# Sparse attention, select stage: key transposes of the next gathered batch behind the scores, second query pair behind them, division by the sums one batch later

## What is computed

```python
I = jnp.einsum('bth,bhts->bts', iw, logits)      # index scores of every token pair
I = jnp.where(causal, I, NEG)
vals, idx = jax.lax.top_k(I, TOPK)               # 32 keys per token
valid = vals > NEG / 2
q = (x @ wq).reshape(B, S, H, hd)                # 16 heads of 128
k = x @ wk                                       # one key and one value per token
v = x @ wv
k_sel, v_sel = gather(k, idx), gather(v, idx)
scores = jnp.einsum('bthd,btkd->bhtk', q, k_sel) * hd ** (-0.5)
scores = jnp.where(valid[:, None], scores, NEG)
p = jax.nn.softmax(scores, axis=-1)
o = jnp.einsum('bhtk,btkd->bthd', p, v_sel)
return o.reshape(B, S, H * hd) @ wo
```

## Time and profile before

| | |
|---|---|
| three runs | 3225.93, 3227.54, 3230.31 us; median 3227.54 |
| the profiled execution's own time | 3237.2 us |
| its span, first to last instruction | 3235.4 us |
| TensorE busy over the span | 2675.0 us (83%) |
| VectorE, ScalarE, GpSimd busy | 1769.7 (55%), 1487.8 (46%), 1052.4 us (33%) |
| mean granted TensorE clock | 0.911 |
| the loop of the select stage | about 2320 to 3058 us |

### The profile page before, as it was taken

One profiled execution on the slowest core, in us unless ns is written; L12 is line 12 of the kernel. 1 busy time (PEld: TensorE's weight loads), 2 busy tenths in 40 slices (PEclk: granted clock), 3 DMA queues, 4 the chain that ended last, 5 costly groups with the idle time before them and its releaser, 6 DMA issues. The chain is left out here.

```text
span 3235.4 us, 41872 instructions
## 1 busy us (share of the span) xinstructions
PE 2675.0 (83%) x14686; PEld 2043.5 (63%) x14686; DVE 1769.7 (55%) x3107; ACT 1487.8 (46%) x2915; POOL 1052.4 (33%) x943
## 2 busy tenths in 40 slices
PE   4967899899899895867989898888587877887788
PEld 4755455555555554756867676777576766766577
DVE  6456755656646736455357989898222233333443
ACT  2435457456456452333249868687333333233232
POOL 2542212102103101542314424242344445555222
PEclk9988999999999995988989999999788888899799
DMA  4241000000000003240010000000222222222100
GB/s 136 77 132 40 7 14 21 10 27 8 15 21 13 4 1 106 73 129 19 0 40 1 1 7 1 7 1 8 100 64 66 63 69 79 70 75 81 63 1 26
DMA packets 68367, 135.42 MB, mean 42 GB/s; under 512 B 16720, under 2 KB 38056, under 8 KB 66896
## 3 DMA queue, kind: packets, MB, share of 16 engines
q0 software_dynamic: 26048, 70.91, 7.4%
q1 hardware_dynamic: 42128, 61.96, 5.8%
HBM read 113.73 MB, written 18.71 MB: 41 GB/s over the span
## 5 line engine op out<-in xcount | busy, mean ns | idle before, releaser
L2138 POOL DMA_INDIRECT KV<-kv_scratch,sidx x384 | 368.3, 959 | 384.8 <-PE ps L2011 198.3
L1347 ACT ACTIVATE PT<-ps 128x512 f32<-128x512 f32 (+3 forms) x640 | 313.2, 534 | 321.3 <-PE ps L1098 178.9
L1213 DVE TENSOR_REDUCE xn<-ps 128x1 f32<-128x1024 f32 (+7 forms) x384 | 332.5, 907 | 112.6 <-PE ps L1074 85.9
L35 PE MATMUL ps<-KIh,qih 128*128 128x512 f32 (+2 forms) x640 | 252.6, 395 | 64.2 <-DVE Isc L1766 37.3
L36 PE MATMUL ps<-KIl,qih 128*128 128x512 f32 (+2 forms) x640 | 243.9, 381 | 0.0
L37 PE MATMUL ps<-KIh,qil 128*128 128x512 f32 (+2 forms) x640 | 243.4, 380 | 0.0
L1766 DVE SCALAR_TENSOR_TENSOR Isc<-ps,iw,Isc 128x1024 f32<-128x1024 f32 (+7 forms) x216 | 208.7, 966 | 56.5 <-ACT ps L1679 50.8
L1095 PE MATMUL ps<-qB,KB 128*128 128x512 f32 (+2 forms) x640 | 237.8, 372 | 0.0
L1679 ACT ACTIVATE ps<-ps,iwa 128x1024 f32<-128x1024 f32 (+7 forms) x240 | 198.0, 858 | 65.2 <-PE ps L37 64.5
L2114 DVE TENSOR_REDUCE smx<-ps 128x4 f32<-128x512 f32 (+3 forms) x92 | 61.0, 663 | 259.8 <-PE ps L1990 134.7
L2065 ACT ACTIVATE sP<-ps,snm 128x128 f32<-128x128 f32 (+2 forms) x256 | 101.2, 405 | 218.0 <-DVE snm L2117 170.0
(11 more groups left out here) (349 smaller groups left out, 7170.4 us busy)
## 6 DMA issues: line engine op xcount, KB each, us to landing
cs<-in_rope SPq DMA_DIRECT2D x20, 512.0 KB, 4.3
w1raw<-in_w SPq DMA_DIRECT2D x16, 512.0 KB, 4.1
ycomb<-y_rows SPq DMA_DIRECT2D x16, 512.0 KB, 4.9
KV<-kv_scratch,sidx POOLq DMA_INDIRECT x384
w2raw<-in_w SPq DMA_DIRECT2D x16, 256.0 KB, 5.2
xn_rows<-xnr SPq DMA_DIRECT2D x8, 512.0 KB, 4.1
whr<-in_whead SPq DMA_DIRECT2D x16, 256.0 KB, 3.0
wir<-in_wi SPq DMA_DIRECT2D x1, 2176.0 KB, 8.2
```

Of the source, the lines that this page charges most:

```text
L35: pe.matmul(out, lhs[0], rhs[0], start=start, stop=False)
L1213: v.tensor_reduce(mp[:, CT * h + r, k:k + 1], o[:, 0:end], AX_X, ALU.max).then_inc(a_free, 1)
L1347: s.activation(PT[:, rnd % 2, hh, lo:CH], ps[:, ST_BANKS[e % 3], lo:CH], ACT.Exp, scale=SCALE).then_inc(a_exp, 1)
L2138: g.indirect_dma_start(KV[:, BG * (k % RB) + m, :], None, a["kv_scratch"], bass.IndirectOffsetOnAxis(sidx[:, t % 2, at:at + 1], 0)).then_i ...
```

## The change

Three edits, in the loops of three engines.

- The key transposes become a function `turn_keys(batch)`. The first gathered batch's are made ahead of the loop; those of every other one are made in the iteration before its own (`after(n_)` gives the next batch if it is gathered), behind the scores and ahead of the output and of the product with the values. On ScalarE the two copies into `KT` (`turned_keys`) move in the same way, behind the exponentials of the iteration before and ahead of the copy into `oT`.
- Where a batch has two query pairs, the second is computed behind the scores and behind the key transposes, and on ScalarE copied behind the exponentials.
- On VectorE the reciprocal and the multiplications of batch `n_ - 1` stand in iteration `n_`, behind the copy into `sPT` and ahead of the maximum of batch `n_`.

```diff
--- before.py
+++ after.py
@@ -1914,6 +1914,9 @@
         def landed(batch):
             return 1 + 2 * GNUM[batch]
 
+        def after(n_):
+            return BATCHES[n_ + 1] if n_ + 1 < NBAT and BATCHES[n_ + 1][0] == "G" else None
+
         def w_piece(m):
             return slice(NHQ // 2 * m, NHQ // 2 * (m + 1))
 
@@ -1956,17 +1959,19 @@
                 queries(PAIRS[k], 6 + k % 2)
             pe.wait_ge(s_w[0], 32)
             pe.wait_ge(s_qe, FIRST_PAIRS)
+            def turn_keys(batch):
+                g = GNUM[batch]
+                pe.wait_ge(s_g[g % RB], 16 * BG * (g // RB + 1))
+                pe.wait_ge(s_kte, landed(batch))
+                for k in range(BG):
+                    i = pe.transpose(ps[:, k // 4, (k % 4) * P:(k % 4 + 1) * P], KV[:, BG * (g % RB) + k, 0:P], ident[:])
+                    if k % 4 == 3:
+                        i.then_inc(s_kt, 1)
+
+            turn_keys(BATCHES[0])
             for n_ in range(NBAT + LAG + 1):
                 batch = BATCHES[n_] if n_ < NBAT else None
                 old = n_ - LAG
-                if batch and batch[0] == "G":
-                    g = GNUM[batch]
-                    pe.wait_ge(s_g[g % RB], 16 * BG * (g // RB + 1))
-                    pe.wait_ge(s_kte, landed(batch))
-                    for k in range(BG):
-                        i = pe.transpose(ps[:, k // 4, (k % 4) * P:(k % 4 + 1) * P], KV[:, BG * (g % RB) + k, 0:P], ident[:])
-                        if k % 4 == 3:
-                            i.then_inc(s_kt, 1)
                 if 0 <= old < NBAT:
                     count, wide = groups(BATCHES[old])
                     pe.wait_ge(s_p, old + 1)
@@ -1974,7 +1979,7 @@
                     for j in range(count * wide // P):
                         i = pe.transpose(ps[:, 4, j * P:(j + 1) * P], sP[:, old % (LAG + 1), j, :], ident[:])
                     i.then_inc(s_pt, 1)
-                for pair in PAIRS_AT.get(n_, []):
+                for pair in PAIRS_AT.get(n_, [])[0:1]:
                     pe.wait_ge(s_qe, PAIR_NO[pair])
                     queries(pair, 6)
                 if batch:
@@ -2000,6 +2005,11 @@
                             pe.matmul(o, qD[:, h0 + h, P * (t % 2):P * (t % 2 + 1)], dK[:, 0:wide], start=h == 0, stop=False)
                             i = pe.matmul(o, far[:], dmb[:, 0:wide], start=False, stop=h == count - 1)
                         i.then_inc(s_s, 1)
+                if after(n_):
+                    turn_keys(after(n_))
+                for pair in PAIRS_AT.get(n_, [])[1:]:
+                    pe.wait_ge(s_qe, PAIR_NO[pair])
+                    queries(pair, 6)
                 for t in OUT_AT.get(n_, []):
                     output(t)
                 if 0 <= old < NBAT:
@@ -2044,16 +2054,18 @@
 
             for k in range(FIRST_PAIRS):
                 queries(PAIRS[k], 6 + k % 2)
+            def turned_keys(batch):
+                for k in range(2):
+                    s.wait_ge(s_kt, landed(batch) + k + 1)
+                    if GNUM[batch] >= 1:
+                        s.wait_ge(s_s, NUMBER[GATHERED[GNUM[batch] - 1]] + 1)
+                    s.copy(KT[:, 4 * k:4 * k + 4, :], ps[:, k, :]).then_inc(s_kte, 1)
+
+            turned_keys(BATCHES[0])
             for n_ in range(NBAT + LAG):
                 batch = BATCHES[n_] if n_ < NBAT else None
                 old = n_ - LAG
-                if batch and batch[0] == "G":
-                    for k in range(2):
-                        s.wait_ge(s_kt, landed(batch) + k + 1)
-                        if GNUM[batch] >= 1:
-                            s.wait_ge(s_s, NUMBER[GATHERED[GNUM[batch] - 1]] + 1)
-                        s.copy(KT[:, 4 * k:4 * k + 4, :], ps[:, k, :]).then_inc(s_kte, 1)
-                for pair in PAIRS_AT.get(n_, []):
+                for pair in PAIRS_AT.get(n_, [])[0:1]:
                     queries(pair, 6)
                 if batch:
                     count, wide = groups(batch)
@@ -2065,6 +2077,10 @@
                         i = s.activation(flat[:, wide * m:wide * (m + 1)], ps[:, 2 + n_ % 2, wide * m:wide * (m + 1)], ACT.Exp,
                                          bias=snm[:, at, m:m + 1], scale=SSC, accum_out=ssum[:, at, m:m + 1])
                     i.then_inc(s_ex, 1)
+                if after(n_):
+                    turned_keys(after(n_))
+                for pair in PAIRS_AT.get(n_, [])[1:]:
+                    queries(pair, 6)
                 if 0 <= old < NBAT:
                     last = BATCHES[old]
                     t = last[1]
@@ -2106,21 +2122,24 @@
                     v.wait_ge(s_pt, old + 1)
                     v.wait_ge(s_o, old)
                     v.tensor_copy(sPT[:, 0:count * wide // P, :].rearrange("p m k -> p (m k)"), ps[:, 4, 0:count * wide]).then_inc(s_pte, 1)
+                if 1 <= n_ < NBAT + 1:
+                    count, wide = groups(BATCHES[n_ - 1])
+                    at = (n_ - 1) % (LAG + 1)
+                    flat = sP[:, at].rearrange("p m k -> p (m k)")
+                    v.wait_ge(s_ex, n_)
+                    v.reciprocal(srs[:, at, 0:count], ssum[:, at, 0:count]).then_inc(s_rs, 1)
+                    v.wait_ge(s_rs, n_)
+                    for m in range(count):
+                        i = v.tensor_scalar(flat[:, wide * m:wide * (m + 1)], flat[:, wide * m:wide * (m + 1)], srs[:, at, m:m + 1], None, ALU.mult)
+                    i.then_inc(s_p, 1)
                 if batch:
                     count, wide = groups(batch)
                     at = n_ % (LAG + 1)
-                    flat = sP[:, at].rearrange("p m k -> p (m k)")
                     v.wait_ge(s_s, n_ + 1)
                     v.tensor_reduce(smx[:, at, 0:count], ps[:, 2 + n_ % 2, 0:count * wide].rearrange("p (m k) -> p m k", k=wide), AX_X,
                                     ALU.max).then_inc(s_nm, 1)
                     v.wait_ge(s_nm, 2 * n_ + 1)
                     v.tensor_scalar(snm[:, at, 0:count], smx[:, at, 0:count], -SSC, None, ALU.mult).then_inc(s_nm, 1)
-                    v.wait_ge(s_ex, n_ + 1)
-                    v.reciprocal(srs[:, at, 0:count], ssum[:, at, 0:count]).then_inc(s_rs, 1)
-                    v.wait_ge(s_rs, n_ + 1)
-                    for m in range(count):
-                        i = v.tensor_scalar(flat[:, wide * m:wide * (m + 1)], flat[:, wide * m:wide * (m + 1)], srs[:, at, m:m + 1], None, ALU.mult)
-                    i.then_inc(s_p, 1)
                 for t in OUT_AT.get(n_, []):
                     v.wait_ge(s_y, OUT_NO[t] + 1)
                     v.tensor_tensor(X[:, t, :], ps[:, 7, 0:D], X[:, t, :], ALU.add).then_inc(s_x, 1)
```

## The result

Four runs of each: 3207.5 us (3201.4 to 3210.7) against 3228.9 (3225.9 to 3233.7); ratio 0.9942, interval 0.9914 to 0.9971. The change is faster by 18.7 us, between 9 and 28, where 64 were forecast. The time lies in the range, near rival (a); three tenths of the forecast gain came.

The account below looks back on a forecast made before the run. TensorE was taken as nearest to the bound in the select loop, leaking through idle time, low clock and stalls. From 3237.2 us, -43 -10 -8 +12 -15 = -64 gave 3173.2, or 3163.5 against the runs' median; range 3110 to 3215.

Parts of the forecast that it names:

- rival (a): Select loop: TensorE's wait moves to the gather, at +47 and no clock gain; 3213 us, chance 15%.
- part 4: Key transposes want gathered rows earlier; perhaps eight more batches late by 1.5 us each: +12 us, bounds 0 and +47.
- three signs of being wrong: Over 60 us of DMA waits, clearly more "remote" waits, or over 30 us new before gathered scores for the KT copy.
- part 1: Dense product's wait for VectorE's copy shrinks; -43 us after 8 off for the last eight gathered batches, bounds -53 and -20.
- part 2: Second query pair behind the scores finds ScalarE's copy done: eight times 1.2 us, -10 us, bounds -27.3 and 0.
- part 3: TensorE's smaller waits, for the mask and before output products, shrink: -8 us, bounds -21 and 0.
- part 5: TensorE's clock spends less time at the lower level as idle time falls: -15 us, bounds -40 and 0.
- Rival (b): Slower: late key transposes hold up an output and a product needing no gathered row; 3269.5 us, chance 7%.
- Rival (c): Nothing: time saved between two stalls is given back in the next; within 6.5 us of 3227.5, chance 6%.
- Rival (d): The clock comes back as well, at -40, with larger savings on TensorE's waits: -113 us, 3114.5 us, chance 17%.

Follow-up runs that it names:

- e9: The whole change, but with key transposes behind the output product instead of ahead of it: 3215.1 us against 3225.3 for the kernel before, ratio 0.9967.
- e16: The kernel before with only the division moved one batch later: 3208.0 us against 3226.7, ratio 0.9938.
- e6: The whole change, unchanged, run where the kernel before takes 3068.4 us: 3107.1 us, ratio 1.0121.
- e10 to e12: Whole change, transposes behind output, last query pair behind value product; then also old division, or earlier first four gathers: 3226.2, 3228.8, 3229.7 us against 3225.3.
- e5: The kernel before, unchanged, profiled again where it takes 3068.4 us: 3070.3 us, ratio 1.0004.
- e15: The kernel before with each indirect gather exchanged for a plain DMA of 128 rows (output differs): 3051.9 us against 3226.7, ratio 0.9468.

## Why the prediction was wrong

The step that failed is part 4, the gather: +12 forecast, +53 measured. Two of the prediction's three signs of being wrong appeared, over 60 us of DMA waits (61.1) and clearly more "remote" waits (83 to 130 us); the third, a new wait before the gathered scores, stayed at 14.3 us. TensorE's idle time by line gives the terms as they came, in the first pair of traces (dense product, L35, outputs and mask, key transposes, gathered scores):

| term | forecast | measured |
|---|---|---|
| part 1, copy ahead of division | -43 | 61.1 to 8.2: -53 |
| part 2, second pair | -10 | 27.3 to 10.9: -16 |
| part 3, small waits | -8 | 14.3 to 5.7 and 8.2 to 5.8: -11 |
| part 4, gather | +12 | 7.7 to 61.1: +53 |
| part 5, clock | -15 | 0.87 to 0.87: 0 |
| not foreseen, gathered scores | 0 | 10.4 to 14.3: +4 |
| sum | -64 | -23 (stage -28, runs -19) |

**Parts 1 to 3 were right as waits**, in mechanism and nearly in size; part 1 came out at its far bound of -53. What I deducted from it for the last eight batches was not lost there. As time they did not come: the division alone is worth 19 us under A and 5 under B, and only with half the gather does the whole change give 36.

**Part 4 is the step that failed.** It was outside even its bound of +47, and it failed in three places. First, the slack was read from one pair: 5.4 us between landing and use, in a pair that a stall had stretched. Under B, where nothing is stalled, before already waits 18.9 us for the gather in 12 batches; the undisturbed pair of the earlier trace rows, 9.1 us from one gathered batch's last score product (2607.17) to the next one's (2616.30 in the earlier trace rows), is shorter than the 10 us that GpSimd issues a batch in, and I did not compare these two numbers. Second, the distance that the transposes moved was wrong: an output is 16 products in 32 records, 124.0 / 16 = 7.7 us, and I called it "3 to 4 at the upper level"; under B at a clock of 0.97 the 16 outputs take 114.3 us, 7.1 each. A third of the batches want their rows not 4 but 8 us earlier, more than the 5.4 us of slack. e9, with the transposes behind the output, has 45.8 us of DMA waits under A against 61.1 (its time is not better, though). Third, the stalls of the earlier trace rows were taken as independent of the gather. They end when it lands (33 of 39 late steps in the changed kernel). Where TensorE waited for VectorE 4 us after such a landing, the transposes in the gap wait for the same landing: saving that wait only uncovers the gather's. How the 53 us divide among the three no run tells.

**Part 5**, -15 forecast, came to nothing in the whole change: the idle time only shrank by a sixth, and the DMA waits are as long as those that went. At such a place the transposes of 2646.98 run at 1.97 us, the lower level. Under B the clock even fell by 0.03. In e16, where the key transposes stand in their old place and wait 7.6 us, it did rise, to 0.90. The Trainium skill, "TensorE: Matmul & The Clock Gate", section on the PE-mode transpose, says that transposes don't count as busy in the same way. By that sentence this term would be near 0, the right number here; no run tells whether for its reason.

**Rival (a)** described what happened: 3213 forecast, 3207.5 measured, with the gather's +47 as +53; that the total is so close is partly luck, since parts 1 to 3 were larger by 19 us than it had them. It had 15% because GpSimd's 198 us of waiting for TensorE were read as slack. Part of it was none: in 15 of 45 batches of before GpSimd stood some 2.4 us, 37 us in all, although the product that frees the slot had ended before its last issue. Under B this happens once. **Rival (b)**, slower through the same mechanism, is what the change does under B; its point of decision, a mean lateness of 1.3 us over 47 batches, is about where e6 stands: 84.3 - 19.8 = 64.5 us, 1.4 us each, while the savings there are 37 us and not the 61 that it was set against. **Rival (c)** had a part of the truth: the "remote" waits before the maximum rose from 83 to 130 us, and e10 to e12 changed waits without changing the time. **Rival (d)** didn't come.

## What to carry to other kernels

Before work that waits for a DMA is moved earlier, compare the period of the loop where nothing disturbs it with the period of the transfer that feeds it: 9.1 us of TensorE against 10 us of issuing meant that in such pairs a gain on TensorE would meet the gather. Halving a suspected feeder (at the price of a wrong output) gave in one pair of runs what the waits did not: -36 us for the change with half the gather, +39 with the whole. And a wait that is filled by work with another dependence has to be checked for both ending at the same event.

## What the runs showed of the hardware

- The same program runs at 3068 or at 3225 to 3243 us, by conditions outside of it (B and A), and a change of order can have opposite signs in them (1.0121 against 0.9942).
- Under A many of TensorE's releases come late. Of 92 batches of scores, 33 (before) and 39 (changed) have their semaphore step over 1 us after the recorded end of the matmul, mostly 2 to 6 us, at the landing of the indirect gather in flight; of the 48 query pairs in the loop, whose copies ScalarE makes, 24 and 26. Under B none does. Half the indirect DMAs, or plain ones of the same bytes, remove 160 or 175 us of 3227 under A; the half removes only 28 under B.
- GpSimd needs 0.95 to 0.96 us for an indirect DMA of 128 rows (e5, before) and 0.55 for a plain one (e15); eight indirect ones take 9.7 us, and their rows land 1.8 to 1.9 us later.
